# C products of a scan on GpSimd, its D term and residual on TensorE, and attention masks written by ScalarE

## What is computed

```
def step(h, inp):
    u_t, d_t, B_t, C_t = inp
    dA = jnp.exp(d_t[..., None] * A)
    h = dA * h + (d_t * u_t)[..., None] * B_t[:, None, :]
    y = jnp.sum(h * C_t[:, None, :], axis=-1)
    return (h, y)
y = jnp.transpose(ys, (1, 0, 2)) + xc * Dskip
y = y * jax.nn.silu(z)
return y @ out_w.T
...
scores = jnp.where(allowed, scores, NEG)          # local: dist > 0 and dist <= 128
attn = jax.nn.softmax(scores, axis=-1)            # causal: tril
```

## Time and profile before

| | |
|---|---|
| time, median of 3 runs | 6355.99 us (6347.57 to 6366.04) |
| the profiled execution's own time | 6365.0 us |
| its span, first to last instruction | 6363.1 us |
| PE busy | 5155.9 us, 81% |
| DVE busy | 4310.5 us, 68% |
| POOL busy | 3250.2 us, 51% |
| ACT busy | 2866.6 us, 45% |
| mean granted TensorE clock | 0.891 of 2.4 GHz |

### The profile page before, as it was taken

One profiled execution on the slowest core, in us unless ns is written; L12 is line 12 of the kernel. 1 busy time (PEld: TensorE's weight loads), 2 busy tenths in 40 slices (PEclk: granted clock), 3 DMA queues, 4 the chain that ended last, 5 costly groups with the idle time before them and its releaser, 6 DMA issues. The chain is left out here.

```text
span 6363.1 us, 79030 instructions
## 1 busy us (share of the span) xinstructions
PE 5155.9 (81%) x22250; PEld 2583.2 (41%) x22314; DVE 4310.5 (68%) x6171; ACT 2866.6 (45%) x4845; POOL 3250.2 (51%) x2383
## 2 busy tenths in 40 slices
PE   4888888888886897778977999954897799974897
PEld 1333333333332343534433555422664344442564
DVE  4999999999998474054765777752675566652675
ACT  4665665655654354233543555521332344431232
POOL 2788888888886252023523444317333455526333
PEclk8999999999999897578988999966998899986898
DMA  1224211211211000000002333222454333302455
GB/s 71 80 99 146 102 56 78 80 55 79 80 60 53 0 0 0 0 0 0 0 7 55 87 84 83 52 81 74 159 189 139 81 90 92 90 1 72 152 187 177
DMA packets 175518, 476.34 MB, mean 75 GB/s; under 512 B 29888, under 2 KB 55232, under 8 KB 147392
## 3 DMA queue, kind: packets, MB, share of 16 engines
q1 hardware_dynamic: 156992, 434.35, 21.4%
q0 software_dynamic: 18176, 37.79, 1.7%
HBM read 364.94 MB, written 107.07 MB: 74 GB/s over the span
## 5 line engine op out<-in xcount | busy, mean ns | idle before, releaser
L337 POOL TENSOR_TENSOR mamba_bu<-mamba_du,mamba_b_all 128x1024 f32<-128x1024 f32 x512 | 1200.3, 2355 | 282.5 <-DVE mamba_hc L599 270.2
L592 DVE TENSOR_TENSOR_SCAN mamba_bu<-psum,mamba_bu 128x512 f32<-128x512 f32 x1024 | 1194.2, 1208 | 157.6 <-ACT psum L529 124.9
L428 PE MATMUL psum<-mamba_hc,consts 128*128 128x512 f32 x2048 | 1019.0, 622 | 31.7 <-DVE mamba_du L604 28.6
L529 ACT ACTIVATE psum<-mamba_delta,A 128x510 f32<-128x510 f32 x1024 | 684.6, 685 | 571.4 <-DVE mamba_bu L592 556.8
L599 DVE TENSOR_TENSOR mamba_hc<-mamba_bu,psum 128x1024 f32<-128x1024 f32 x512 | 612.9, 1197 | 6.5 <-PE psum L419 4.5
L1597 POOL DMA_INDIRECT results<-ffn_moe_y_rows,ffn_moe_row_of x312 | 302.1, 968 | 506.3 <-DVE ffn_moe_y_rows L1787 430.7
L428 PEld LDWEIGHTS psum<-mamba_hc,consts 128*128 128x128 f32 x2048 | 404.2, 199 | 371.3 <-issue 351.0
L1712 ACT ACTIVATE ffn_moe_act<-ffn_moe_act 128x512 f32<-128x512 f32 x344 | 217.0, 631 | 719.9 <-DVE ffn_moe_act L1756 719.8
L2140 POOL TENSOR_TENSOR loc_q_bd<-loc_q_max,weights_l1a 128x512 fp32r<-128x512 f32 x256 | 274.8, 1102 | 416.8 <-DVE loc_q_max L2376 409.1
L419 PE MATMUL psum<-mamba_parts,consts 128*128 128x512 bf16 x448 | 177.6, 396 | 329.3 <-DVE mamba_hc L599 327.1
L2367 DVE TENSOR_REDUCE cau_top<-psum 128x2 f32<-128x512 f32 (+1 forms) x384 | 263.3, 692 | 212.0 <-PE psum L2207 198.8
(11 more groups left out here) (405 smaller groups left out, 11343.4 us busy)
## 6 DMA issues: line engine op xcount, KB each, us to landing
mamba_b_all<-b_rows SPq DMA_DIRECT2D x128, 1024.0 KB, 8.2
ffn_moe_w_gu<-gate_up_parts SPq DMA_DIRECT2D x78, 1024.0 KB, 4.8
pairs<-empty_rows SPq DMA_DIRECT2D x6, 3432.0 KB, 15.4
ffn_moe_got<-pairs SPq DMA_DIRECT2D x78, 264.0 KB, 3.2
ffn_moe_w_down<-in_l_moe SPq DMA_DIRECT2D x78, 256.0 KB, 2.9
qk_rows<-loc_qk SPq DMA_DIRECT2D x16, 1024.0 KB, 8.4
ffn_moe_back<-results SPq DMA_DIRECT2D x32, 512.0 KB, 4.8
qk_rows<-cau_qk SPq DMA_DIRECT2D x16, 1024.0 KB, 4.3
```

Of the source, the lines that this page charges most:

```text
L337: nc.gpsimd.tensor_tensor(bu[:, J % BU, :, :], du[:, q % 2, :, :], b, ALU.mult).then_inc(bu_ready, 1)
L428: nc.tensor.matmul(ysum[h], mem.ident, hc[:, J % HC, h, :], start=(n == 0), stop=(n == NST - 1), skip_group_check=True).then_inc(summed, 1)
L529: nc.scalar.activation(by_seq(dA[i % DECAYS])[:, :, 1:S], by_seq(delta[:, q % 2, h, :])[:, :, 1:S], ACT.Exp, scale=mem.A[:, q % 2, h * NST ...
L592: nc.vector.tensor_tensor_scan(bu[:, J % BU, h, :], dA[i % DECAYS], bu[:, J % BU, h, :], 0.0, ALU.mult, ALU.add).then_inc(scanned, 1)
```

## The change

In the scan stage:

- The C products of steps 2 and 7 of each unit go to POOL (`POOLED_C`), three steps late. Their C rows come by DMA from rows that are stored with the B rows. The product is now written in place into `bu`, which has 8 buffers; `hc` is gone. Chunks of two B rows rotate through four places.
- The reductions come four steps late (`LATE` = 3), and a drive waits for the reduction of its buffer.
- The D term is two matmuls with a diagonal matrix (`skip`) into `ysum`. `gated` becomes one product of `ysum` (PSUM) and z on DVE, in step 4; POOL's gate is gone. The residual is added by a matmul of X with the identity, and ACT writes X itself.
- The front work moves on PE and on ACT, as the orders below show; ACT's softplus is spread over steps 11 to 14.

In the attentions, ACT writes the mask of a diagonal block of keys into the bank behind the exp that has read it, and PE adds the scores to it without a mask matmul (`seeds`). The first two units of each attention and the other mask of the local attention keep theirs.

TensorE, from the last step of one unit through the first steps of the next, before: each of steps 0 to 3 has a C row, a reduction and half a convolution (`L388`).

The diff, cut to its core:

```diff
+                for h in range(HALVES):
+                    nc.vector.tensor_scalar(mem.skip[:, d, h, :], mem.ident, w["D_" + c][:, h:h + 1], None, ALU.mult)
...
-    CHUNK = 4
-    BU, HC, DECAYS = 4, 3, 3
+    CHUNK, SLOTS = 2, 4
+    CHUNKS = NST // CHUNK
+    BU = 8
+    LATE = 3
+    DECAYS = 3
+    POOLED_C = (2, 7)
...
-            return [("conv", q, 0), ("conv", q, 1), ("out", q - 2, 0), ("xdbl", q, 0), ("dt", q, 0), ("dt", q, 1), ("gate", q, 0), ("gate", q, 1)]
+            return [("conv", q, 0), ("conv", q, 1), ("xdbl", q, 0), ("out", q - 2, 0), ("dt", q, 0), ("dt", q, 1), ("gate", q, 0), ("gate", q, 1)]
...
-                sp.dma_start(b_rows[q % 2], xdbl[32:32 + NST, :]).then_inc(b_stored, 16)
-                sp.wait_ge(b_stored, 16 * (q + 1) + LEAD)
-                for c in range(NST // CHUNK):
-                    if q >= 1:
-                        sp.wait_ge(bu_ready, NST * (q - 1) + CHUNK * (c + 1) + LEAD)
+                sp.dma_start(b_rows[q % 2], xdbl[32:32 + 2 * NST, :]).then_inc(bc_stored, 16)
+                sp.wait_ge(bc_stored, 16 * (q + 1) + LEAD)
+                sp.wait_ge(weighed_pool, len(POOLED_C) * (q - 1) + LEAD)
+                chosen = b_rows[q % 2, NST + POOLED_C[0]:NST + POOLED_C[1] + 1:POOLED_C[1] - POOLED_C[0], :]
+                sp.dma_start(c_rows[:, q % 2, :, :], chosen.unsqueeze(0).to_broadcast([D, len(POOLED_C), T])).then_inc(c_landed[q % 2], 16)
+                for c in range(CHUNKS):
+                    chunk = q * CHUNKS + c
+                    sp.wait_ge(bu_ready, CHUNK * (chunk - SLOTS + 1) + LEAD)
...
-                pool.wait_ge(hc_ready, J - BU + 1 + LEAD)
+                pool.wait_ge(summed, J - BU + 1 + LEAD)
...
-                pool.wait_ge(z_ready, q + 1 + LEAD)
+            def weigh(J):
+                pool.wait_ge(scanned, 2 * J + 2 + LEAD)
...
-                for h in range(HALVES):
-                    pool.wait_ge(y_step, 2 * q + h + 1 + LEAD)
...
-                    nc.gpsimd.tensor_tensor(du[:, d, h, :], du[:, d, h, :], z[:, d, h, :], ALU.mult).then_inc(y_ready, 1)
...
-            def out(q):
-                pool.wait_ge(work_read, position["out", q, 0] + 1 + LEAD)
+                q, n = J // NST, J % NST
+                pool.wait_ge(c_landed[q % 2], 16 * (q // 2 + 1) + LEAD)
...
-                nc.gpsimd.tensor_tensor(X[:, tokens(q)], X[:, tokens(q)], outp[:, :], ALU.add).then_inc(added, 1)
+                c = c_rows[:, q % 2, POOLED_C.index(n), :].unsqueeze(1).to_broadcast([D, 2, T])
+                nc.gpsimd.tensor_tensor(bu[:, J % BU, :, :], bu[:, J % BU, :, :], c, ALU.mult).then_inc(weighed_pool, 1)
...
-                    if n == 5 and q >= 1:
-                        gate(q - 1)
-                    if n == 10 and q >= 1:
-                        out(q - 1)
...
+                    if J >= LATE and by_pool(J - LATE):
+                        weigh(J - LATE)
...
-            gate(UNITS - 1)
-            out(UNITS - 1)
+            for J in range(NST * UNITS - LATE, NST * UNITS):
+                if by_pool(J):
+                    weigh(J)
...
-            def spread_c(q, n):
-                J = NST * q + n
+            def spread_c(J):
+                q, n = J // NST, J % NST
+                if by_pool(J):
+                    return
...
-                pe.wait_ge(hc_ready, J + LEAD)
+                pe.wait_ge(weighed_vector, vector_until[J] + LEAD)
...
-                pe.wait_ge(hc_ready, J + 1 + LEAD)
...
-                    pe.wait_ge(y_step, 2 * q + LEAD)
+                    pe.wait_ge(y_ready, q + LEAD)
+                    for h in range(HALVES):
+                        nc.tensor.matmul(ysum[:, h, :], mem.skip[:, d, h, :], u[:, d, h, :], start=True, stop=False, skip_group_check=True)
+                if by_pool(J):
+                    pe.wait_ge(weighed_pool, pool_until[J + 1] + LEAD)
+                else:
+                    pe.wait_ge(weighed_vector, vector_until[J + 1] + LEAD)
...
-                    nc.tensor.matmul(ysum[h], mem.ident, hc[:, J % HC, h, :], start=(n == 0), stop=(n == NST - 1),
-                                     skip_group_check=True).then_inc(summed, 1)
+                    last = nc.tensor.matmul(ysum[:, h, :], mem.ident, bu[:, J % BU, h, :], start=False, stop=(n == NST - 1),
+                                            skip_group_check=True)
+                last.then_inc(summed, 1)
...
+                pe.wait_ge(y_ready, q + 1 + LEAD)
...
-                    pe.wait_ge(y_ready, 2 * q + h + 1 + LEAD)
-                    last = nc.tensor.matmul(to, mem.out_proj[:, q % 2, h, :], du[:, q % 2, h, :], start=(h == 0), stop=(h == 1))
-                last.then_inc(work_ready, 1)
+                    nc.tensor.matmul(to, mem.out_proj[:, q % 2, h, :], du[:, q % 2, h, :], start=(h == 0), stop=False, skip_group_check=True)
+                nc.tensor.matmul(by_seq(to), mem.ident, in_time(by_seq(X[:, tokens(q)]), q), start=False, stop=True, skip_group_check=True).then_inc(work_ready, 1)
...
-                    spread_c(q, n)
-                    if NST * q + n >= 1:
-                        reduce(NST * q + n - 1)
-                    if n < 4 and more:
-                        convolve(q + 1, n // 2, n % 2)
-                    if n == 5 and q >= 1:
+                    spread_c(NST * q + n)
+                    if NST * q + n >= LATE + 1:
+                        reduce(NST * q + n - LATE - 1)
+                    if more:
+                        if n == 0:
+                            convolve(q + 1, 0, 0)
+                        if n == 1:
+                            convolve(q + 1, 0, 1)
+                            convolve(q + 1, 1, 0)
+                        if n == 2:
+                            convolve(q + 1, 1, 1)
+                        if n == 5:
+                            project_u(q + 1)
+                    if n == 6 and q >= 1:
...
-                        if n == 7:
-                            project_u(q + 1)
-                        if n in (9, 10):
-                            project_dt(q + 1, n - 9)
-                        if n in (12, 13):
-                            project_gate(q + 1, n - 12)
-            reduce(NST * UNITS - 1)
+                        if n in (7, 8):
+                            project_dt(q + 1, n - 7)
...
+                            project_gate(q + 1, n - 11)
+            for J in range(NST * UNITS - LATE - 1, NST * UNITS):
+                reduce(J)
...
-                dve.wait_ge(c_ready, J + 1 + LEAD)
-                dve.wait_ge(summed, 2 * (J - HC + 1) + LEAD)
+                dve.wait_ge(c_ready, vector_until[J + 1] + LEAD)
...
-                nc.vector.tensor_tensor(hc[:, J % HC, :, :], bu[:, J % BU, :, :], c_bc.unsqueeze(1).to_broadcast([D, 2, T]), ALU.mult).then_inc(hc_ready, 1)
+                nc.vector.tensor_tensor(bu[:, J % BU, :, :], bu[:, J % BU, :, :], c_bc.unsqueeze(1).to_broadcast([D, 2, T]), ALU.mult).then_inc(weighed_vector, 1)
...
-                for h in range(HALVES):
-                    dve.wait_ge(summed, 2 * NST * (q + 1) - 1 + h + LEAD)
-                    nc.vector.scalar_tensor_tensor(du[:, q % 2, h, :], u[:, q % 2, h, :], w["D_" + DIRS[q % 2]][:, h:h + 1], ysum[h],
-                                                   ALU.mult, ALU.add).then_inc(y_step, 1)
+                dve.wait_ge(summed, NST * (q + 1) + LEAD)
+                dve.wait_ge(z_ready, q + 1 + LEAD)
+                nc.vector.tensor_tensor(du[:, q % 2, :, :], ysum, z[:, q % 2, :, :], ALU.mult).then_inc(y_ready, 1)
...
-                    if J >= 1:
+                    if J >= 1 and not by_pool(J - 1):
...
-                    if n == 1 and q >= 1:
+                    if n == LATE + 1 and q >= 1:
...
+        t_seeds = [seeds[s % QB].get(c) for s in range(STEPS_A) for g, c in t_units(s)]
+        seeds_until = [0, 0, 0]
+        for seed in t_seeds[2:]:
+            seeds_until.append(seeds_until[-1] + (seed is not None))
...
-                pe.wait_ge(powers_ready, number - 1 + LEAD)
...
-                if mask is not None:
+                by_act = number >= 2 and t_seeds[number] is not None
+                if by_act:
+                    pe.wait_ge(seeded, seeds_until[number + 1] + LEAD)
+                else:
+                    pe.wait_ge(powers_ready, number - 1 + LEAD)
+                if mask is not None and not by_act:
...
+                if number + 2 < len(t_seeds) and t_seeds[number + 2] is not None:
+                    act.wait_ge(powers_ready, number + 1 + LEAD)
+                    nc.scalar.activation(mem.bank[T_BANK[number % 2]].rearrange("p (h q) -> p h q", h=GH),
+                                         t_seeds[number + 2].unsqueeze(1).to_broadcast([128, GH, 128]), ACT.Identity).then_inc(seeded, 1)
...
-        stacked_attention(nc, "cau", mem, U, True, masks=[[(0, mem.masks[:, 0, :])], [(1, mem.masks[:, 0, :])]])
```

(2 more changed lines are left out.)

118 lines of the change are left out of this document (69 added, 49 removed).

## The result

The changed kernel takes **6280.7 us** (median of 4 runs, 6276.8 to 6284.4) against 6351.8 us for the kernel before (4 runs, 6346.9 to 6366.0) on the same chip: a ratio of **0.988**, 95% interval 0.987 to 0.990. The forecast was 6270 with a range of 6220 to 6340. The profiled executions have spans of 6278.3 and 6363.1 us, 84.8 us apart.

What follows compares the result with a forecast made beforehand. VectorE's chain was taken to bound the scan stage, TensorE's queue the attentions. From the profiled 6365.0 us, attentions -94 and scan stage +8 gave 6279; that run stood 9 us above the median, hence 6270, range 6220 to 6340.

Steps and rivals of the forecast that it cites:

- VectorE's own work: Scan stage: VectorE's scans and products take 52.65 us a unit, 2.4 less than before, plus 0.4 for hand-overs.
- TensorE at the head: First steps of a scan unit: VectorE waits 1.6 us for step 3's C row and 0.6 at the gate product.
- ACT at the head: First steps of a scan unit: the decay behind ACT's table load comes late, VectorE waits 0.95 us.
- The boundary: Unit's end: the chain over the last Relu, delta, du and POOL's first drive makes VectorE wait 2.0 us a unit.
- The clock: Half clock on the head's matmuls after each unit boundary: 1.6 us more at step 3's product (0 to 2.4).
- so I expect the same dip as before: Unit boundary of the scan stage: TensorE idles 3.3 to 3.5 us and the granted clock falls as before.
- the shorter breaks inside a unit show no dip: Scan stage before the change: the trace shows the clock's dip at the boundary, not in shorter breaks inside a unit.
- The tail and the start: Scan stage's ends: +4 us after the last product, with four reductions before the gate product; +1 us at the start.
- Attention, what TensorE sheds: Both attentions: 508 mask matmuls of 0.22 us leave TensorE, 112 us; ACT's write in their place takes 0.64 us.
- Attention, what is given back: Four-unit attention steps: ACT's sums come 0.45 us late in 32 (14 us); 0.2 in 16 with a high part (3.5 us).
- The first rival: Attentions: ACT bounds the four-unit steps, which don't shorten; 56 of the 112 us are gone, total 6314; chance 0.15.
- The signs: VectorE waiting 2 us for first drive, 3 for step 3's C row; attentions 45 us shorter each; wrong if waits under 4.

Runs made afterwards that it cites:

- two more runs: The changed kernel measured again, ratio 0.989 to the kernel before; and the changed kernel with TensorE writing all attention masks again, ratio 0.996.
- the convolution spread: Changed kernel with the convolution's halves one to a step again (steps 0 to 3): ratio 1.009 to the kernel before, scan stage 2004.6 us.
- products 7 and 11, both kernels: Changed kernel with C products 7 and 11 on POOL in place of 2 and 7: ratio 0.996; the same with softplus one step earlier: 0.995.

## Why the prediction came out right, point by point

- **VectorE's own work.** 52.65 us a unit forecast, and 0.4 for hand-overs. An undisturbed unit is 58.07 us. Counted by slots, as the prediction does, its waits are 1.9, 1.9, 0.6 and 0.9 us (the brackets, which start at the end of a row and not of its slot, give 1.80, 1.66, 0.50 and 0.78). That leaves 52.85. Right; of the 0.4 us half was too much, 6 us in all.
- **TensorE at the head.** 1.66 and 0.50 us against 1.6 and 0.6. Right in place, mechanism and size. The experiment that removes the packing by moving one half ahead removes the wait, and the one that moves a half behind shows the other end, ACT.
- **ACT at the head.** 0.78 against 0.95. Right.
- **The boundary.** 1.8 against 2.0, and moving the Relu one step earlier removes it. Right. POOL is a hair behind: one product more in its queue there, and it takes ACT's place as the last.
- **The clock.** The price of a disturbed head was right (1.6 us), its frequency wrong: 13 of 31 (17 and 15 in two more runs). 18 x 1.6 = 29 us too much, as much as the whole miss of the stage. The step that failed is "so I expect the same dip as before". It held for the kernel before, whose clock fell at all 31 boundaries, and it didn't carry over to a pause of nearly the same length (3.23 against 3.15 us). Why it fell in 13 cases and not in 18 stays open. The kernel before could have warned me: in 9 of its 31 units the clock also fell behind a pause of 2.2 us in step 8, and in the others it didn't. So the prediction's sentence that the shorter breaks inside a unit show no dip is wrong. The Trainium skill ("TensorE: Matmul & The Clock Gate", on the oscillation in real kernels) has each burst after a long enough break start cold. Taken as literally as in the prediction, the kernel before agrees with it at its boundaries (31 of 31), and the changed kernel doesn't: eighteen heads ran at full clock behind the same pause of 3.23 us.
- **The tail and the start.** +3.2 and +0.9 against +4 and +1.
- **Attention, what TensorE sheds.** 107 against 112 us; ACT's write at 0.60 us against 0.64. Right.
- **Attention, what is given back.** 56 us (107 shed, 51.6 kept) against 17.5: this term failed. All of its 17.5 us were ACT's late sums, which measured 17, and it had nothing else. Missing were VectorE's maxima in the local attention (15.3 us of waits, 27 us of time when relieved), the bank behind the four-unit steps (5.4), the hand-overs behind VectorE's reads (10) and some 10 us that no row names. The first rival, that four-unit steps don't shorten, had 56 of the 112 us lost, and 56 is what was lost. For the attentions that rival's number, not the forecast, was right (its total of 6314 should have been 6308 by its own terms). Its reason wasn't: it gave ACT 6.3 of 6.4 us in such a step, and the trace has 6.1 of 7.9 in the local attention and 5.2 of 7.2 in the causal one. In the local attention it was VectorE. In the causal one the order of ACT's work is what the experiment moved about without a gain, and what holds its four-unit steps stays open in part.
- **The signs.** The waits were where they were looked for, save that the clock's part came at the scan of step 4 and not at the C row of step 3. The attentions got 20 and 32 us shorter, not 45 each, with ACT at 77 and 78% and not 85. VectorE's waits are 4.8 us a unit, above the 4 that would have meant wrong.
- **Unchanged code.** -14 us that no step had, from the granted clock in the feed-forward stage. It differed by 12 us between two runs of the changed kernel.

## What to carry to other kernels

When work is moved off the engine that bounds a stage, lay out every other engine that has more than three quarters of the stage busy, not only the one that receives the work; here that was VectorE in the local attention, and three small operations moved off it, on top of the masks, were worth more than the masks of that stage (27 against 20 us). A pause of the matmul engine at a boundary is a place to put work that stands in a full stretch right behind it: here it cost at most 0.2 us a unit there, it freed the head, and the clock stayed up. And when a total agrees with a forecast, compare it stretch by stretch, since errors of 29 and 42 us can hide in it.

## What the runs showed of the hardware

- The same pause with the same work before it (3.23 us idle) is followed by half clock in some units and not in others: 13, 17 and 15 of 31 in three traces of the same scan stage. Other pauses at the boundary: 3.15 us, 31 of 31 (kernel before); 3.23 us, 31 of 31 with product 7 alone on POOL and 29 of 31 with the convolution spread; 4.15 us, 31 of 31 (products 7 and 11, both kernels); 1.34 us, or 1.72 with half a convolution before it, none. A pause of 2.2 us in step 8 of the kernel before: 9 of 31. What decides in the mixed cases no run shows.
- Such a head is 1.6 us longer in the changed kernel, so four more of them are 6 us between two runs of it, whose scan stages differ by 5.3 us.
- A pooled or moved operation can thus change the time through the clock alone; with product 7 alone on POOL nearly all of the loss is of this kind by the count above.
- ACT writes a 128x512 bank from a bfloat16 tile of constants, repeated over four heads, in 602 ns, about what its exp from PSUM takes (591).
- Of two chains that end at the same point only the later shows: with the Relu earlier the boundary's wait fell from 1.8 us to nothing, and with one product more on POOL it was 2.7 us whether the Relu was early or not.
